# Interleaving the inner and outer matmuls of a long convolution, and an earlier low part on VectorE

## The reference, cut to what matters

```python
x = x + conv31(group_norm(x)) + bias      # one 31x31 filter per channel
x = x + conv11(group_norm(x))             # one 11x11 filter per channel, made from 4 points
```

## Time and profile before

| | |
|---|---|
| median of 3 runs | 3515.29 us |
| the profiled execution's own time | 3515.18 us |
| its span | 3513.4 us |
| TensorE matmul busy | 3427.3 us (98%) |
| TensorE weight load busy | 3265.2 us (93%) |
| VectorE busy | 3146.1 us (90%) |
| ScalarE busy | 1299.3 us (37%) |
| GpSimd busy | 1202.2 us (34%) |
| mean granted TensorE clock | 0.995 of full speed |

### The profile page before, as it was taken

How to read it: one execution, slowest core, us unless ns; L and a number is a source line. 1 busy time by engine, 2 the same in 40 slices (tenths; PEclk the granted TensorE clock), 3 DMA queues, 4 the chain that set the end, 5 groups by cost and what they waited for, 6 DMA issues and landing times.

```text
span 3513.4 us, 66359 instructions
## 1 busy us (share of the span) xinstructions
PE 3427.3 (98%) x21312; PEld 3265.2 (93%) x21312; DVE 3146.1 (90%) x4671; ACT 1299.3 (37%) x1637; POOL 1202.2 (34%) x840
## 2 busy tenths in 40 slices
PE   5899999999999999999999999999999999999997
PEld 4789999999999999999999999999999999999996
DVE  7899998899988999988999988999989999889988
ACT  3333333333333333333333333333333333333333
POOL 6213333333333333333333333333333333333332
PEclk9999999999999999999999999999999999999999
DMA  8998888898888898888898898988888988889774
GB/s 181 187 200 160 172 161 166 175 181 166 163 169 168 165 177 171 160 165 173 172 173 169 161 166 173 184 165 163 169 168 163 182 168 160 165 170 186 136 147 89
DMA packets 896128, 587.51 MB, mean 167 GB/s; under 512 B 501656, under 2 KB 858136, under 8 KB 895576
## 3 DMA queue, kind: packets, MB, share of 16 engines
q1 hardware_dynamic: 895416, 585.62, 86.3%
q10 hardware_dynamic: 544, 0.38, 0.1%
HBM read 499.20 MB, written 86.61 MB: 167 GB/s over the span
## 4 chain that ended last, share of the span: by engine, by line
PE 92%; issue 3%; SPq 2%; DVE 2%; DMA 1%; POOL 0%; ACT 0%; DVEq 0%; POOLq 0%; ACTq 0%
PE acc L1302 92%; SPq L554 2%; DMA toep<-padded 1%; DVE yt L1088 0%; DVE acc L1079 0%; DVE raw L1097 0%; DMA padded<-raw 0%; DVE x_lo L1062 0%; ACT toep L953 0%; DVE x_lo L1056 0%; SPq L568 0%; SPq L594 0%; DVE raw L1134 0%; SPq L578 0%; DVE acc L1119 0%
## 5 line engine op out<-in xcount | busy, mean ns | idle before, releaser
L1302 PE MATMUL acc<-x_hi,toep 128*112 128x224 f32 (+5 forms) x14208 | 3303.6, 323 | 79.1 <-DMA toep<-padded 70.4
L1302 PEld LDWEIGHTS acc<-x_hi,toep 128*112 128x112 f32 x14208 | 2381.1, 182 | 188.6 <-issue 79.9
L1302 PE MATMUL acc<-x_lo,toep 128*112 128x224 f32 (+5 forms) x7104 | 2299.4, 324 | 0.0
L1302 PEld LDWEIGHTS acc<-x_lo,toep 128*112 128x112 f32 x7104 | 1289.7, 182 | 52.2
L793 POOL TENSOR_TENSOR xt<-xt 128x960 f32<-128x960 f32 x188 | 425.7, 2264 | 1118.9 <-DVE xt L1037 1118.9
L830 ACT ACTIVATE x_hi<-xt 128x768 fp32r<-128x768 f32 (+1 forms) x384 | 279.2, 727 | 1092.4 <-POOL xt L789 578.7
L1079 DVE TENSOR_TENSOR acc<-acc,yt 128x896 f32<-128x896 f32 x384 | 418.9, 1091 | 220.6 <-PE acc L1302 219.5
L788 POOL TENSOR_TENSOR xt<-xt 128x512 f32<-128x512 f32 x180 | 233.1, 1295 | 1094.5 <-DVE xt L1037 1094.5
L833 ACT ACTIVATE x_hi<-xt 128x960 fp32r<-128x960 f32 x384 | 386.9, 1007 | 572.3 <-POOL xt L793 323.1
L1037 DVE STREAM_TRANSPOSE xt<-images 128x960 f32<-128x960 f32 x384 | 452.5, 1178 | 34.8 <-ACT images L817 6.6
L817 ACT ACTIVATE images<-raw,norm 128x896 f32 (+1 forms) x384 | 439.8, 1145 | 88.1 <-DVE norm L1017 88.1
(11 more groups left out here) (59 smaller groups left out, 412.7 us busy)
## 6 DMA issues: line engine op xcount, KB each, us to landing
toep<-padded SPq DMA_DIRECT2D x384, 322.0 KB
toep<-padded SPq DMA_DIRECT2D x384, 273.0 KB
toep<-padded SPq DMA_DIRECT2D x384, 217.0 KB
out_dram<-raw SPq DMA_DIRECT2D x189, 336.0 KB, 5.6
raw<-in_x_dram SPq DMA_DIRECT2D x93, 672.0 KB, 11.7
toep<-padded SPq DMA_DIRECT2D x768, 58.5 KB
toep<-padded SPq DMA_DIRECT2D x384, 80.5 KB
toep<-padded SPq DMA_DIRECT2D x384, 47.2 KB
```

Of the source, the lines that this page charges most:

```text
L1302: last = nc.tensor.matmul(dst, stationary, src[:, cols], start=(m == matrices[0][0] and part == 0 and src is x_hi), stop=(m == matrices[-1 ...
```

## The change: what it does

Two edits. In the long slots of VectorE's program, `low` moves up to stand right behind `low_inner`, ahead of the end of the normalisation chain and of `add_residual`; `add_residual` becomes the last. In TensorE's program the matmuls of a job are first listed and then issued: in a long job all 36 inner ones alternate with the first 36 outer ones (inner, outer, inner, outer), and 12 outer ones follow. A long job's waits for `lo_ready` and `image_ready` therefore stand ahead of its first matmul. Short jobs keep their order. The instructions are the same in number and shape.

```diff
@@ VectorE, a long slot
                         if after and not low_first:
                             low_inner(*after)
-                        if not low_first:
-                            add_residual(i, s)
+                        if after and not low_first:
+                            low(*after)
                         if early2:
                             normalisation_ends(norm2_ordinal(group2), norm2, normalised)
                         if early1:
                             normalisation_ends(i * 2 + 1, norm1, job(i, LAST_FIRST) + 1)
-                        if after and not low_first:
-                            low(*after)
-                        if low_first:
-                            add_residual(i, s)
+                        add_residual(i, s)
@@ TensorE, convolve
-                for k, (bank, column, start, shift, held, count, matrices) in enumerate(f.products()):
-                    if k == before_outer:
-                        pe.wait_ge(lo_ready, n + 1)
-                        if positive(n + 1 - P_RING):
-                            pe.wait_ge(image_ready, n + 1 - P_RING)
...
+                products = [list(steps(k, *product)) for k, product in enumerate(f.products())]
+                outer_steps = [x for product in products[before_outer:] for x in product]
+                alone = 0 if f.halved else len(products[:before_outer])
+                beside = [x for product in products[alone:before_outer] for x in product]
+                for product in products[:alone]:
+                    for x in product:
+                        multiply(*x)
+                pe.wait_ge(lo_ready, n + 1)
+                if positive(n + 1 - P_RING):
+                    pe.wait_ge(image_ready, n + 1 - P_RING)
+                for k, x in enumerate(outer_steps):
+                    if k < len(beside):
+                        multiply(*beside[k])
+                    multiply(*x)
```

More of the change, by code:

```diff
@@ L1283, in convolve, with steps @@
                 before_outer = 3 if f.halved else 1
-                for k, (bank, column, start, shift, held, count, matrices) in enumerate(f.products()):
-                    if k == before_outer:
-                        pe.wait_ge(lo_ready, n + 1)
-                        if positive(n + 1 - P_RING):
-                            pe.wait_ge(image_ready, n + 1 - P_RING)
+                def steps(k, bank, column, start, shift, held, count, matrices):
                     def outputs(m):
@@ L1298, in convolve, with multiply @@
                         for part, src in ((0, x_hi), (0, x_lo), (1, x_hi)):
[L1299 to L1306, removed]
+                            yield (dst, w, part, src[:, cols], m == matrices[0][0] and part == 0 and src is x_hi,
+                                   m == matrices[-1][0] and part == 1, done[k])
+                def multiply(dst, w, part, moving, first, last, signal):
+                    block = last_place(i, s)
+                    stationary = (toeplitz(toep, f, place_of_toep, part, w) if block is None
+                                  else last_toeplitz(block, part, w))
+                    ins = nc.tensor.matmul(dst, stationary, moving, start=first, stop=last, skip_group_check=True)
+                    if last and signal is not None:
+                        ins.then_inc(signal, 1)
+                products = [list(steps(k, *product)) for k, product in enumerate(f.products())]
[12 more added lines that the diff above has]
+                    multiply(*x)
             def iteration(i):
```

## The result

The changed kernel takes 3525.03 us (median of 11 runs, 3523.99 to 3527.68) against 3516.00 us for the kernel before (11 runs beside it and earlier, 3513.63 to 3516.78). The ratio is 1.0027, with a 95% interval of 1.0019 to 1.0035: about 9 us slower, clear of no change. The forecast said 3517 us with a range of 3490 to 3535; the number is the one of rival B (3524 for its smallest form), which had 0.34. Both terms that made up the forecast were off.

A forecast was written before the change was run, and what follows sets the result against it. The prediction took the distance between starts of neighbouring matmuls on TensorE as the bound. From 3515.2 us, -6.5 (pace) + 7.5 (slot 6) + 1.1 (start-up) gave 3517.3, say 3517 us; range 3490 to 3535, the forecast's own 3509 to 3522.

The forecast's parts named there:

- rival B: Slower: the wait ahead of slot 6's first matmul stands and alternation gains nothing; 3524 to 3537 us, put at 3527; chance 0.34.
- TensorE's distances set the end: From the start-up on, only shorter distances between starts of neighbouring matmuls on TensorE help, and only a new wait hurts.
- A narrow matmul between two wide ones: In long jobs, the wide successor's load starts with the narrow matmul and must finish first; a pair costs 0.30, now 0.305.
- Rival A: In long jobs, the load of a narrow matmul's successor is hidden: 37 us less pace time, 3493 us; chance 0.27.
- The pair gains 0.001 us: Alternation in long jobs: 36 pairs in each of 180 jobs gain 0.001 us each, 6.5 us less (bounds 0 to 32).
- A change of PSUM bank costs nothing: Alternating matmuls in long jobs: 72 bank changes a job taken as zero; at 0.001 us each, 13 us as upper end.
- Slot 6's wait: TensorE waits 0.26 us for slot 4's late `low` before slot 6's long job, 29 times: 7.5 us (bounds 0 to 17).
- The reorder is needed: VectorE's earlier `low` in slot 4 saves 0.6 us of slot 6's wait against the old order behind this alternation.
- Start-up: In iteration 1 the job at 245.66 waits for `low` until 246.74: 1.1 us, once.
- Signals: Later `p2_done` and `u_done` in long jobs cost zero, hidden by VectorE's idling for `conv_done`; without that cover 0.6 us a job.

## Why the prediction was right or wrong

The range held the time, but in part by luck. The likeliest case was no clear change, and the result is 0.27% slower, which rival B had. Against the sum's 3517.3 us the pace was wrong by some 13 us one way, and the wait of slot 6 by 5.5 and the start-up by 0.8 the other way. By its steps:

- *TensorE's distances set the end, and a change in its waits or its pace is the whole effect.* Right: 106.68 to 106.99 us, split into 0.24 of pace and 0.07 of wait, carries 8.7 of 9.2 us.
- *A narrow matmul between two wide ones has the load of its successor on its back.* Right, and shown by the shortened loads in both kernels. Rival A, from the reorder window in the Trainium skill ("TensorE: Matmul & The Clock Gate", section "The mechanism"), did not happen here: the trace shows one load ahead and not two (no load starts before the matmul ahead of it has), and 36 pairs take 10.49 us against 10.46 for the same matmuls in the old order. The changed kernel's loads for this, at the second matmul of slot 8 and at the start of the 12 that stand alone (10.39 us for 71 matmuls, plus 0.10 for the first):

```profile
1708.42 0.39 PEld L1300 LDWEIGHTS acc<-x_lo,toep 128*112 128x112 f32 x2
...
1718.81 0.18 PEld L1300 LDWEIGHTS acc<-x_lo,toep 128*112 128x112 f32 x1
```

- *The pair gains 0.001 us: -6.5 us.* Wrong, the term that failed. It measured +0.24 us an iteration, about +7 us. The rows showed one narrow matmul behind a wide one at 0.10 and I took a part of that for all 36. They do gain it: 102 ns among wide ones against 104. But the wide neighbours give it back and more: 448 columns take 205 ns where they took 201, 384 take 177 and not 174, 352 take 162 and not 160. One neighbour in a trace shows one side of the exchange.
- *A change of PSUM bank costs nothing, 13 us at most.* The term I set to zero is the one that fits best in sign. But 48 changes among wide matmuls cost 26 ns a job, 24 by blocks 27, 24 among narrow ones 7, and 72 with pairs 33. No single price gives these, so I don't call the bank the cause.
- *Slot 6's wait: 29 x 0.26 = 7.5 us.* Right place, wrong size: 0.07 us, 2 us in all. Without alternation it is 0.16. Errors stand against each other. The 0.39 us that VectorE would be late is 0.19, as the transpose in slot 2 comes 0.18 earlier and with it the high part that `low` waits for: ScalarE's rounding (L833) ends 15.82 us behind the start of slot 2's long job and not 16.03. The notice is 0.3 and not 0.23. And the jobs of slots 2 to 5 are 0.08 us longer in the changed kernel, which hides that much of the stall.
- *The reorder is needed.* Right in direction, far too small where I gave it 0.6 us in slot 6: all six long slots would stall, and in most iterations the clock would fall twice.
- *Start-up: 1.1 us.* It is 0.35 in the changed kernel. With the new order alone iteration 2 starts 1.1 us earlier than before, and its start in the profiles of the other kernels spreads over 3 us, so this term can't be judged.
- *Signals.* Right: the combination never sets an end. In slot 10 it starts at 10.48 instead of 10.35 us and VectorE still idles for `conv_done`; the wait for it stands at 228.8 us in total against 219.5.

So rival B's number was met with B's wait at about a quarter of its size and a pace loss that only its upper form held. What stays open is the mechanism behind the 33 ns in a long job. The 7 ns of the untouched short jobs lie in their first three or nine steps, so they come from the long job ahead; how it passes them on is open too. Whether the place of the operands in memory has a part in either wasn't tested.

## What to carry to other kernels

A weight load is a debt of the matmul before it: a matmul too narrow to cover the next load costs that load, whatever comes next. So mixing narrow with wide ones won nothing here, where all loads have 112 columns; fewer weight columns behind the narrow ones did (14 ns for each of 192 columns). Moving a wait to the front of a stage uses up slack that no view of waits shows; compute the low end of that slack for each slot, and include the first load, which then has nothing to hide under. When effects are of a few ns a matmul, compare the length of a loop iteration inside the profiles, not the medians, and look whether a change reaches matmuls that it didn't touch.

## What the runs showed of the hardware

- After a stall of TensorE of about 2 us the granted clock fell to 0.50 (1.2 GHz) within 1.6 us of the restart in 46 of 56 cases, and the job behind it took 13.94 us and not 12.40; in the other 10 it stayed at 1.00.
- A matmul of 192 columns (fp32r) took 104 ns with a weight load of 112 columns behind it and 90 ns with one of 80; no weight load started before the matmul ahead of it had.
- The order of matmuls whose loads and lengths are the same changed the pace of a long job by 7 to 33 ns in the mean (12.465 us before up to the start of the next job, and up to 12.498), in all five orders tried, and always upwards.
- Each step repeated to 1 ns in 28 iterations, while steps of one width differed by some 8 ns (199 to 208 ns for 448 columns in a short job), and with the alternation in the long job the first three or nine steps of the untouched short job behind it changed.
- A semaphore that VectorE waits for from its own instruction before costs 0.18 us: the next instruction starts 0.10 us behind that one's end, against 0.08 ahead of it.
